# One transfer for the first tile's constants and filters, and a finer first operand, in a convolution and linear-layer kernel

## The reference, cut to what matters

```python
# layer 0: grouped 1-D convolution (4 groups, 9 taps) plus a context per channel, then a linear layer with low-rank experts
conv = conv1d(x, w[64, 16, 9], groups=4, pad=4) + (cond @ c_weight.T)[:, :, None] + fside[None, :, None]
x1   = x + conv @ W.T + b + best_expert(conv)         # W (1024, 1024); softmax gate over 4 ranks, top 1
# layer 1: per-sample mixture of 8 channel matrices, whose weights come from a small network on cond
att  = softmax(gelu(gelu(cond @ W0 + b0) @ W1 + b1) @ W2 + b2)
m    = einsum(att @ weight, x1) + att @ bias_k
out  = x1 + m @ W_base.T + b_base + sum_e sparsemax(router(m))_e * (m @ A_e) @ B_e
```

## Time and profile before

| | us |
|---|---|
| median of 3 runs | 518.55 |
| the runs | 518.16, 518.55, 519.62 |
| the profiled execution | 517.35 |
| its span, first to last instruction | 515.6 |
| PE busy in the span | 506.4 (98%) |
| DVE, ACT, POOL busy | 353.0, 131.4, 142.7 |

### The profile page before, as it was taken

The page is one execution under the profiler, slowest core; times in us unless marked ns, Lnnn a source line. Parts: engine busy times, 40 slices in busy tenths (PEclk is TensorE's granted clock), DMA queues, the critical chain, the costliest instruction groups (busy, mean ns, idle before and its releaser), DMA issues.

```text
span 515.6 us, 8706 instructions
## 1 busy us (share of the span) xinstructions
PE 506.4 (98%) x3227; PEld 478.1 (93%) x3227; DVE 353.0 (68%) x764; ACT 131.4 (25%) x271; POOL 142.7 (28%) x122
## 2 busy tenths in 40 slices
PE   7999999999999999999999899999999999999997
PEld 7999999999999999999999789999999999999986
DVE  2866988847676675766797586685748568584852
ACT  2741343312223122331352221111112111111200
POOL 1000010004443141433113372441606244060620
PEclk9999999999999999999999999999999999999999
DMA  7943404427377564647797952333415233430312
GB/s 273 349 133 125 134 1 135 160 90 239 131 249 229 203 234 158 211 151 258 257 421 268 402 181 85 121 105 127 140 60 165 82 120 106 132 136 18 104 43 81
DMA packets 41382, 85.32 MB, mean 165 GB/s; under 512 B 4059, under 2 KB 25051, under 8 KB 41340
## 3 DMA queue, kind: packets, MB, share of 16 engines
q1 hardware_dynamic: 31884, 61.38, 35.3%
q10 hardware_dynamic: 9456, 23.38, 12.2%
HBM read 59.30 MB, written 25.44 MB: 164 GB/s over the span
## 4 chain that ended last, share of the span: by engine, by line
PE 87%; DMA 7%; DVE 4%; issue 1%; SPq 1%; ACT 0%; POOL 0%; DVEq 0%; ACTq 0%
PE b_x L1178 6%; PE b_x L1180 6%; PE b_x L1181 6%; PE b_m L1129 5%; PE b_p L1162 4%; PE b_p L1164 4%; PE b_p L1163 4%; PE b_y L1178 4%; PE b_y L1181 4%; PE b_y L1180 4%; DMA x_scratch<-xs 4%; PE b_m L1139 2%; PE b_y L1129 2%; PE b_w L1180 2%; PE b_w L1178 2%; PE b_w L1181 2%
## 5 line engine op out<-in xcount | busy, mean ns | idle before, releaser
L530 ACT CAST a_hi<-mixed 128x512 fp32r<-128x512 f32 x64 | 38.7, 620 | 167.1 <-DVE mixed L812 91.8
L479 POOL TENSOR_TENSOR xs<-xs,mixw_sb 128x464 f32<-128x464 f32 (+1 forms) x32 | 45.1, 1419 | 123.7 <-DMA xs<-x_scratch 123.7
L824 DVE TENSOR_TENSOR s_lo<-mixed,s_hi 128x512 fp32r<-128x512 f32 x56 | 64.9, 1180 | 16.6 <-ACT s_hi L542 14.7
L1163 PE MATMUL b_p<-wp_lo,a_hi 128*128 128x232 f32 (+1 forms) x224 | 61.5, 275 | 0.0
L1162 PE MATMUL b_p<-wp_hi,a_hi 128*128 128x232 f32 (+1 forms) x224 | 61.4, 274 | 0.0
L1164 PE MATMUL b_p<-wp_hi,a_lo 128*128 128x232 f32 (+1 forms) x224 | 61.4, 274 | 0.0
L905 DVE TENSOR_TENSOR xs<-b_x,xs 128x464 f32<-128x464 f32 (+1 forms) x58 | 36.1, 622 | 31.1 <-PE b_x L1181 23.9
L542 ACT CAST s_hi<-mixed 128x512 fp32r<-128x512 f32 x56 | 34.8, 622 | 75.8 <-POOL mixed L452 36.2
L817 DVE TENSOR_TENSOR a_lo<-mixed,a_hi 128x512 fp32r<-128x512 f32 x64 | 48.0, 775 | 8.9 <-ACT a_hi L530 8.2
L452 POOL TENSOR_TENSOR mixed<-mixed 128x512 f32<-128x512 f32 x13 | 16.8, 1295 | 118.0 <-DVE a_lo L817 118.0
L1178 PE MATMUL b_x<-wb_hi,s_hi 128*128 128x464 f32 (+1 forms) x112 | 43.0, 384 | 1.7 <-DVE xs L905 1.7
(11 more groups left out here) (237 smaller groups left out, 1198.5 us busy)
## 6 DMA issues: line engine op xcount, KB each, us to landing
blk<-x_scratch SPq DMA_DIRECT2D x16, 512.0 KB, 3.5
blk<-in_xblk SPq DMA_DIRECT2D x15, 516.0 KB, 3.7
xs<-in_x SPq DMA_DIRECT2D x16, 296.0 KB, 4.3
x_scratch<-xs SPq DMA_DIRECT2D x16, 296.0 KB, 3.5
xs<-x_scratch SPq DMA_DIRECT2D x16, 280.0 KB, 3.3
out_dram<-xs SPq DMA_DIRECT2D x16, 280.0 KB, 2.4
w_raw<-in_wcat SPq DMA_DIRECT2D x8, 546.0 KB, 9.9
praw<-in_wcat ACTq DMA_DIRECT2D x8, 464.0 KB, 5.1
```

Of the source, the lines that this page charges most:

```text
L479: pool.tensor_tensor(xs[s][:, a:b], xs[s][:, a:b], bbase[:, a:b], ALU.add).then_inc(x_biased[q], 1)
L530: act.copy(a_hi[:, op, :, :], mixed[:, op, :, :]).then_inc(ahi_done[op], 1)
L824: dve.tensor_tensor(s_lo[:, i, :, :], mixed[:, S_AT[i], :, :], hi(s_hi[:, i, :, :]), ALU.subtract).then_inc(slo_done[i], 1)
L1163: pe.matmul(dst, x_hi, wp_lo[:, k, 0:PLAIN[l]], start=False, stop=False)
```

## The change

- The row constants (now replicated to 128 rows on the host), the contexts' inputs and all filters become one array `front`, 1204 float32 (4816 bytes) on each of 128 partitions, 616 thousand bytes. SP loads it in one transfer, its first. The loads at L318, L319, L321 and L620 go.
- `blk` of tile 0 is loaded whole (4128 bytes a partition) by ACT, as its first transfer; L320 and L322 go from SP's queue. SP's second transfer is now weight chunk 0.
- PE: `keep_warm(11)` in front instead of 7, none between the context product and the convolution, 2 instead of 3 ahead of the weights. The convolution of tile 0 waits for the whole front and the whole `blk`.
- DVE: the large lo part of weight chunk 0 is made ahead of the first context sum, the small one behind it. The second context sum of tile 0 is two operations of 256 elements, one for A11 and one for A12.
- ACT: weight chunks 0 and 1 are both cast ahead of A11. A11 is cast in two pieces, block 0 (128 elements) and blocks 1 to 3 (384 elements). `dense0(0, 0)` waits only for the first piece, `dense0(0, 1)` for both.

```diff
-WARM, WARM_CTX, WARM_WEIGHTS = 7, 1, 3
+WARM, WARM_WEIGHTS = 11, 2
...
+FR_C = ROW
+FR_CW = FR_C + NB
+FR_TAPS = FR_CW + CH
+FRONT = FR_TAPS + GROUPS * 2 * P
...
+        first_in = sb("first_in", [P, FRONT])
+        rw = first_in[:, 0:ROW]
+        filt = first_in[:, FR_TAPS:FRONT].rearrange("p (g c) -> p g c", g=GROUPS)
...
-            sp.dma_start(pk[:, 0:PK_W0], pack[:, 0:PK_W0]).then_inc(s_pk, 16)
-            sp.dma_start(filt[:, 0:half, :], taps[:, 0:half, :]).then_inc(s_filt[0], 16)
-            sp.dma_start(blk[0][:, 0:GROUPS * QX], xblk[0][:, 0:GROUPS * QX]).then_inc(blk_first, 16)
-            sp.dma_start(filt[:, half:, :], taps[:, half:, :]).then_inc(s_filt[1], 16)
-            sp.dma_start(blk[0][:, GROUPS * QX:], xblk[0][:, GROUPS * QX:]).then_inc(blk_loaded[0], 16)
+            sp.dma_start(first_in[:, :], front).then_inc(s_front, 16)
...
-            sp.dma_start(pk[:, PK_W0:], pack[:, PK_W0:]).then_inc(s_mlp, 16)
+            sp.dma_start(pk[:, :], pack).then_inc(s_mlp, 16)
...
-            act.dma_start(rw[:, :], rows.partition_broadcast(P)).then_inc(s_rw, 16)
+            act.dma_start(blk[0][:, :], xblk[0]).then_inc(blk_loaded[0], 16)
             act.dma_start(bk[:, :], bias_k).then_inc(s_bk, 16)
             split_w(0)
-            split_a(A11, 0)
             split_w(1)
+
+            act.wait_ge(sum_done, 1)
+            act.wait_ge(first_sum, 1)
+            act.copy(a_hi[:, A11, 0, :], mixed[:, A11, 0, :]).then_inc(first_hi, 1)
+            act.copy(a_hi[:, A11, 1:, :], mixed[:, A11, 1:, :]).then_inc(ahi_done[A11], 1)
             split_a(A12, 0)
...
-            dve.wait_ge(s_pk, 16)
+            dve.wait_ge(s_front, 16)
...
             dve.wait_ge(ctx_sum, 1)
+            split_w_main(0)
             sum_mix(0, 0)
-            sum_mix(0, 1)
-            split_w(0)
+            split_w_plain(0)
+
+            dve.wait_ge(mix_done, 2)
+            for q in (A11, A12):
+                dve.tensor_tensor(mixed[:, q, :, CH:P],
+                                  mix_bank(0, 1)[:, 4 * CH * q:4 * CH * (q + 1)].rearrange("p (a c) -> p a c", c=CH),
+                                  ctx_row[:, 0:1, CH:P].to_broadcast([P, HK, CH]),
+                                  ALU.add).then_inc((first_sum, sum_done)[q], 1)
             split_a(A11, 0)
             split_w(1)
             split_a(A12, 0)
...
-                if kc == 0:
+                if T == 0 and k == 0:
+                    pe.wait_ge(first_hi, 1)
+                elif kc == 0:
+                    pe.wait_ge(ahi_done[op], g + 1)
+                if T == 0 and k == 1:
                     pe.wait_ge(ahi_done[op], g + 1)
...
-            keep_warm(WARM_CTX)
+            pe.wait_ge(s_front, 16)
             conv_half(0, 0, b_m)
             conv_half(0, 1, b_w)
-            pe.wait_ge(s_pk, 16)
...
+    front = np.concatenate([np.tile(rows, (P, 1)), a["cond_128"].T, a["L0_cond_c_weight"].T,
+                            taps.reshape(P, GROUPS * 2 * P)], axis=1)
```

More of the change, by code:

```diff
@@ L61 @@
 EMB = 128
-WARM, WARM_CTX, WARM_WEIGHTS = 7, 1, 3
-PK_C = 0
-PK_CW = PK_C + NB
-PK_W0 = PK_CW + CH
+WARM, WARM_WEIGHTS = 11, 2
+PK_W0 = 0
 PK_W1 = PK_W0 + EMB
@@ L83, in layer, with build @@
     return g // PAIRS
-def build(nc, x, xblk, taps, wcat0, bcat0, bias0, wcat1, bcat1, b_base, pack, rows, mixw, bias_k, out):
+def build(nc, x, xblk, front, wcat0, bcat0, bias0, wcat1, bcat1, b_base, pack, mixw, bias_k, out):
     x_t = x.rearrange("(t n) c h -> t (n c) h", n=2)
@@ L172, in build @@
         b_m, b_u = bank("b_m"), bank("b_u")
-        s_pk, s_mlp, s_rw, s_bk, s_mixw = sem("s_pk"), sem("s_mlp"), sem("s_rw"), sem("s_bk"), sem("s_mixw")
-        s_filt = [sem("s_filt0"), sem("s_filt1")]
+        s_front, s_mlp, s_bk, s_mixw = sem("s_front"), sem("s_mlp"), sem("s_bk"), sem("s_mixw")
         s_lb, s_bias0, s_bbase = sem("s_lb"), sem("s_bias0"), sem("s_bbase")
@@ L218, in build @@
         consts = sem("consts")
+        first_sum, first_hi = sem("first_sum"), sem("first_hi")
         ctx_terms, ctx_mm, ctx_sum = sem("ctx_terms"), sem("ctx_mm"), sem("ctx_sum")
@@ L727, in _, with split_w_main @@
         def _(dve):
-            def split_w(k):
+            def split_w_main(k):
                 i = (B11, B21)[k // HK]
@@ L733, in split_w, with split_w_plain @@
                                   hi(wb_hi[:, i:i + 2, k % HK, 0:h]), ALU.subtract).then_inc(wlo_done, 1)
+            def split_w_plain(k):
                 dve.wait_ge(whi_done, 2 * k + 2)
-                dve.tensor_tensor(wp_lo[:, k, 0:PLAIN[0]], w_raw[:, k, 2 * h:],
+                dve.tensor_tensor(wp_lo[:, k, 0:PLAIN[0]], w_raw[:, k, 2 * HALF[0]:],
                                   hi(wp_hi[:, k, 0:PLAIN[0]]), ALU.subtract).then_inc(wlo_done, 1)
+            def split_w(k):
+                split_w_main(k)
+                split_w_plain(k)
             def split_t(i, kc):
@@ L916, in take_plain @@
                                   ALU.add).then_inc(finq[s], 1)
[L919 removed]
+            dve.wait_ge(s_front, 16)
             dve.tensor_tensor(u_sb[:, :, :].rearrange("p t (n c) -> p (t n) c", c=CH),
[L921 to L922 removed]
+                              first_in[:, FR_CW:FR_CW + CH].unsqueeze(1).to_broadcast([P, 4, CH]),
+                              first_in[:, FR_C:FR_C + 4].unsqueeze(2).to_broadcast([P, 4, CH]), ALU.mult).then_inc(ctx_terms, 1)
             dve.wait_ge(ctx_mm, 1)
[L924 removed]
             dve.tensor_tensor(ctx_row[:, :, :].rearrange("p t (n c) -> p (t n) c", c=CH),
@@ L1117, in conv_half @@
                 s = T % 2
[L1118 to L1121, removed]
+                pe.wait_ge(blk_loaded[s], 16 * (T // 2) + 16)
                 for g in range(GROUPS):
@@ L1124, in conv_half @@
                     dst = dst_bank[:, :].rearrange("p (a c) -> p a c", c=CH)[:, :, g * GC:(g + 1) * GC]
-                    if T == 0 and n == 0 and g % 2 == 0:
-                        pe.wait_ge(s_filt[g // 2], 16)
                     for side in range(2):
@@ L1270, in network @@
                     pe.wait_ge(s_mlp, 16)
-                    mlp(0, pk[:, PK_C:PK_C + NB])
+                    mlp(0, first_in[:, FR_C:FR_C + NB])
                 if step == 1:
@@ L1325, in _ @@
                       start=True, stop=True).then_inc(ctx_mm, 1)
-            keep_warm(WARM_CTX)
+            pe.wait_ge(s_front, 16)
             conv_half(0, 0, b_m)
             conv_half(0, 1, b_w)
-            pe.wait_ge(s_pk, 16)
             pe.wait_ge(ctx_sum, 1)
-            pe.matmul(b_z[0:NB, 0:CH], pk[:, PK_C:PK_C + NB], pk[:, PK_CW:PK_CW + CH],
+            pe.matmul(b_z[0:NB, 0:CH], first_in[:, FR_C:FR_C + NB], first_in[:, FR_CW:FR_CW + CH],
                       start=True, stop=True).then_inc(ctx_mm, 1)
@@ L1457, in _layout @@
     bias0[0] = bias0[-1] = a["L0_ffn_b"]
-    pack = np.concatenate([a["cond_128"].T, a["L0_cond_c_weight"].T, a["L1_cond_W0"], a["L1_cond_W1"],
-                           a["L1_cond_W2"], a["L1_cond_b0"][:, None], a["L1_cond_b1"][:, None]], axis=1)
+    pack = np.concatenate([a["L1_cond_W0"], a["L1_cond_W1"], a["L1_cond_W2"],
+                           a["L1_cond_b0"][:, None], a["L1_cond_b1"][:, None]], axis=1)
     rows = np.concatenate([a["fside_S_0"], a["L0_ffn_gate_b"], a["L1_cond_b2"], a["L1_ffn_b_router"]])
+    front = np.concatenate([np.tile(rows, (P, 1)), a["cond_128"].T, a["L0_cond_c_weight"].T,
+                            taps.reshape(P, GROUPS * 2 * P)], axis=1)
     mixw = np.zeros((2, OQ, KMIX, MIXES, 2, CH), np.float32)
@@ L1466, in _layout @@
     mixw = mixw.reshape(P, MIXES, 2 * CH)
-    return {"x": x, "xblk": xblk, "taps": taps, "wcat0": wcat0, "bcat0": bcat0, "bias0": bias0, "wcat1": wcat1,
-            "bcat1": a["L1_ffn_lora_B"].reshape(P, D), "b_base": a["L1_ffn_b_base"], "pack": pack, "rows": rows,
+    return {"x": x, "xblk": xblk, "front": front, "wcat0": wcat0, "bcat0": bcat0, "bias0": bias0, "wcat1": wcat1,
+            "bcat1": a["L1_ffn_lora_B"].reshape(P, D), "b_base": a["L1_ffn_b_base"], "pack": pack,
             "mixw": mixw, "bias_k": a["L1_cond_bias_k"]}
```

4 lines of the change are left out of this document (removed).

## The result

The changed kernel takes 515.99 us (median of 22 runs, 514.81 to 519.7) against 518.23 us (median of 22 runs of the kernel before on the same chips, 516.42 to 521.16). The ratio is 0.9961, interval 0.9946 to 0.9976: faster by 0.4%, 2.2 us, where 0.4 us was forecast; the time lies 0.6 us under the range. A second set of 12 runs of it gave 515.96 and 0.996 (0.9934 to 0.9986). The profiled executions differ by less, 515.9 (span 514.2) against 517.35 (span 515.6): 1.45 us.

The account below looks back on a forecast made before the run. PE was taken to bound the kernel, busy 506.4 of 515.6 us. F = 6.2 gave F − 6.63 = −0.4 us, so 517.35 − 0.4 = 516.95 profiled, plus 1.20 to the median: 518.15 us, range 516.6 to 520.0.

Parts of the forecast that it names:

- F: Landing of the front transfer, which everything stands behind: taken as 6.2 us; the time changes by F − 6.63 us.
- the moved split: DVE's large lo part of chunk 0 ahead of the first sum: free if the chunk lands by F + 1.75; expected F + 1.35.
- far end: Upper case for the front's landing: the slow DMA start of the kernel before repeats, giving F = 8.5.
- near end: Lower case for the front's landing: transfers of this shape on idle engines, F = 6.0 or 6.4.
- the way from the A11 sum to chunk 1's lo part: DVE and ACT from tile 0's A11 sum to chunk 1's lo part end: 3.45 us against 3.84, saving 0.4.
- whatever the end of chunk 1's lo part moves by, the end of the kernel moves by: From tile 1's convolution on PE does not stop, so the start's shift reaches the end whole, if later inputs are ready.
- The prediction's own sign: A span that moves by more than tile 1's convolution moves was to show the forecast wrong.
- the 1.20 us from the profiled execution to the median: Added to the profiled execution's forecast of 516.95 us to give the median of 518.15 us.
- something else moves: Rival: PE's waits behind 120 us shift, either way, by 2 us or so: 516.5 or 520.5 us; chance 0.13.
- The 4 added warm matmuls lie in time in which PE waits for F anyway: PE's start: the added warm matmuls cost nothing unless the front lands before 5.4 us.
- With both queues in use no slice passes 428 GB/s: Reading of the before trace: queues share the DMA engines, so `blk` on ACT's queue brings no extra bandwidth.
- the fit that the prediction took from the Trainium skill: First transfers: 2.0 us plus bytes over 436 GB/s, giving 4.6 us for the pair, F = 5.4, gain 1.2 us.

Follow-up runs that it names:

- order-only kernel: The kernel before with the changed kernel's DVE and ACT order and pieces, its own transfers and warm matmuls kept: 518.85 us, ratio 1.0017 (0.9999 to 1.0036).
- transfers-only: The changed kernel with its transfers and warm matmuls, but the DVE and ACT order, whole sum and whole cast of before: 516.74 us, ratio 0.9967.
- seven-warm: The changed kernel with 7 warm matmuls in front in place of 11: 517.8 us, ratio to before 0.9997 (0.9968 to 1.0026).
- plain-rows: The kernel before with the row constants stored as 128 rows in HBM instead of one row broadcast in the read: 517.22 us, ratio 0.998.
- broadcast-back: The changed kernel with the old broadcast read issued by ACT ahead of `blk`, into an unused tile: 523.49 us (6 runs), ratio to before 1.0103.
- before again: The kernel before, unedited, run again for a second profiled execution: 517.46 us.
- after again: The changed kernel, unedited, run again for a second profiled execution and more times: 515.96 us, ratio to before 0.996 (0.9934 to 0.9986).
- `blk` on SP: The changed kernel with tile 0's `blk` issued by SP right behind the front instead of by ACT: 516.21 us, ratio to before 0.9967 (0.9941 to 0.9992).
- Closing the gap of before: The kernel before with 4 warm matmuls between context product and convolution in place of 1: 517.34 against 519.23 us, ratio 0.9971 (0.9948 to 0.9995).
- the candidate: The changed kernel with `blk` on SP behind the front, first context sum ahead of chunk 0's split, small lo part behind the second sum: 515.37 us, ratio 0.9939.
- widened before: The kernel before without its one warm matmul between context product and convolution: 519.36 against 518.75 us, ratio 1.0007 (0.9984 to 1.0029).

## Why the prediction was wrong, step by step

**Right.** PE bounds the kernel, and tile 1's convolution follows the end of chunk 1's lo part: both moved by 1.13 us, and up to 132 us PE kept that shift whole (−1.15 to −1.18). The context product took 6.85 − 6.31 = 0.54 us (0.5 forecast), the convolution started at 6.85 = F + 1.04 (F + 1.03), and the moved split was free: DVE's first split started at 8.38 (limit 9.5), and DVE then waited only 0.27 us, for PE. That this holds only while the chunk comes early was right too, by the order-only kernel.

**Mis-sized: F.** 6.2 was forecast, 5.81 measured (5.79 again; 5.69 and 6.02 in the transfers-only and seven-warm kernels, whose first transfers are the same). The forecast stood between transfers on idle engines and the ramp of the kernel before, and no row said what made that ramp. The plain-rows and broadcast-back kernels say it: mainly the broadcast read, though with it F was 6.7 and not the 8.5 of the far end. Without it the near end holds (6.0) and a little more. Worth 0.4 us.

**Mis-sized: the way from the A11 sum to chunk 1's lo part.** 3.45 forecast, 3.23 measured. Up to the start of `a_lo` it was 1.26 us (10.62 to 11.88) for the 1.30 of the sum. The difference lies behind it: `a_lo` and chunk 1's lo parts took 1.97 us (11.88 to 13.85) where their durations sum to 2.13, because each operation's row starts before the row ahead of it has ended (`a_lo` from 11.88 for 0.69, chunk 1's large lo part at 12.49). The rows of before had the same overlap, 4.26 us of durations in 3.84 us, and the prediction called it small and left it out of the new sum. The A11 sum itself started at 10.62 instead of F + 4.90 = 10.71. Worth 0.3 us. Together: −0.4 − 0.4 − 0.3 = −1.1, which is the 1.13 us of the traces.

**Failed: "whatever the end of chunk 1's lo part moves by, the end of the kernel moves by".** The sum put everything behind the start at nothing. F and the way alone would have left it at 518.55 − 1.1 = 517.4, inside its range; it left the range by this step and by the next. The prediction's own sign says so: the span moved by more than tile 1's convolution, by 1.46 us (514.16 against 515.62) where the convolution moved by 1.13. The 6.3 us of idle time behind 120 us are not spread either: in before 2.7 us lie around the turn of the layers near 293 us, and 3.4 follow PE's last matmul. The turn moved. PE's windows around it, in before, before again, after, after again:

```profile
280.00:320.00 40.00, 37.33 (x221) 33.82 (x220) 28.37 (x50) 9.94 (x18) 17.45 (x12) 1.00 0.67 253
```
```profile
280.00:320.00 40.00, 37.30 (x219) 33.63 (x218) 28.11 (x49) 9.96 (x18) 17.47 (x12) 1.00 0.67 250
```
```profile
280.00:320.00 40.00, 38.03 (x224) 34.39 (x223) 25.98 (x49) 9.66 (x17) 16.91 (x12) 1.00 0.64 241
```
```profile
280.00:320.00 40.00, 37.95 (x223) 34.40 (x223) 26.00 (x48) 9.54 (x17) 16.83 (x12) 1.00 0.63 237
```
PE stands 2.7 us there in before, twice, and 2.0 in after, twice, and the shift goes from −0.73 to −1.35 and from −1.06 to −1.69 across it: 0.6 us that the sum lacked. Elsewhere after lost a little. In its first profile PE waits at 141 us for DVE, which it doesn't do in before, and the shift falls from −1.18 to −0.70; in the second it falls by 0.1:

```profile
141.22 1.86 PEld L1139 LDWEIGHTS b_z<-first_in,blk 128*128 128x128 f32 x16 [0.55 <-DVE xs L914]
```
What at the turn makes PE wait less in after isn't settled; the kernels with the new transfers stand 1.6 to 2.2 us there, the seven-warm one with its late start too (1.7), except broadcast-back (2.8) and `blk` on SP (3.8, with the clock fallen); those with the old transfers stand 2.5 to 2.7, and with the new order alone it is 3.2.

**Failed: the 1.20 us from the profiled execution to the median.** The forecast of 518.15 carried them over from 3 runs of before; in after the median is 0.09 us above the profiled execution. That is half of the miss of 2.16 us, and the profiled execution (516.95 forecast, 515.9 measured) the other half. With 22 runs the 1.20 is 0.88 in before, so one profile of each kernel shows 0.8 us less than the medians do. Fewer executions with a fallen clock in after are one reason, told next; the rest can be the choice of executions.

**Partly right: the rival "something else moves".** It was given 0.13 and had 2 us either way with nothing but the waits for it. It names the waits, not the clock, which has a part of its own: the mean granted clock that each run lists is below 0.9985 in 46 of the 104 runs of before that list one, which take 519.6 us on average against 517.9 for the others, and in 5 of 34 of after.

**Wrong, though not what the sum missed: "The 4 added warm matmuls lie in time in which PE waits for F anyway".** They do lie there, but what they prevent has a price. The sum counted on them for the context product's 0.5 us and gave the convolution its full pace, and both came true; it saw no cost beyond that without them. Taking four matmuls away from after costs 2.1 us at the start of the trace and 1.8 us of the median (516.0 to 517.8). Closing the gap of before brought about 0.3%, just clear of nothing. The Trainium skill, page TensorE: Matmul & The Clock Gate, section "HAM oscillation — how this bites in real kernels", tells of a wait for a DMA after which PE starts slow again. The trace agrees in the broadcast-back kernel, whose last warm loads took 0.11 us each and whose matmuls after the wait for `blk` took 3.75 us for 16 at a clock of 0.50. The seven-warm kernel is another case, since it was slow from its first load on. The same page of the Trainium skill says that a kernel shows a different number of slow first matmuls from one execution to the next. The warm loads agree, since the kernels give PE the same work up to there: the same 22 took 4.71 us in after (4.77 again), 4.35 in transfers only, 3.89 in the candidate.

**Two readings of the prediction that don't hold.** "With both queues in use no slice passes 428 GB/s" rests on a trace in which ACT's queue carried 44 KB, all but done when the rate was high. The trace of after does show it: with the front and `blk` in flight in two queues no slice up to their landings passes 403 GB/s. And the fit that the prediction took from the Trainium skill, page DMA: Bandwidth & Descriptors, stands there in the section "Anatomy of one DMA — SWDGE (gpsimd) path": it is for transfers on GpSimd's path, while this kernel's are issued by SP and ACT. The estimate by it was F = 5.4; measured was 5.81.

**Where the 2.2 us are.** The means of the runs that list a clock are 518.67 before (104) and 516.51 after (34). More runs of before with a fallen clock: the means of the runs above 0.9985 alone differ by 517.93 − 516.10 = 1.8, so about 0.3. That 1.8 is near what the profiled executions, whose clock at the turn had not fallen, show: their spans are 515.6 and 515.7 before, 514.2 and 513.8 after, 1.7 apart on average. Of it the start is 1.0 to 1.1 and the turn 0.6 to 0.7, less the 0.1 to 0.5 at 141 us. A start that is slow in some executions of before isn't needed for this account and isn't shown; 3 of the 29 runs of after with a full mean clock took 519.1 to 519.7 us too, and what slowed them has no records. The interval of the ratio is 0.8 us either way, so nothing finer can be read from the times.

## What to carry to other kernels

A wait of PE for its first inputs isn't free time: fill it with matmuls until the real ones start, and judge that by medians, because one profile can show the lucky execution. A change at the start can move a wait far behind it: compare the same instruction at several places of both traces, not at the start alone. Replicate small constants in HBM rather than broadcast them in the read, above all ahead of the first large loads. Here work moved ahead of a queue's urgent operation lost time without the transfer that brings its input early; time both, and each alone.

## What the runs showed of the hardware

- A read of one HBM row (336 bytes) into 128 partitions took 5.0 us in before and 6.1 in the broadcast-back kernel, 2.1 with 128 rows in HBM, and slowed the transfers of the other queue too: 48 to 92 GB/s instead of 184 to 324 between 2 and 4.5 us.
- The granted clock reads 1.00 from the first microsecond, while 128-wide loads take 0.22 us and later ones 0.12. It reads 1.00 from 7 to 11 us in the seven-warm kernel too, where 16 matmuls took 3.39 us. The end of the slow time, an estimate from the 22 warm loads at these two paces, was about 3.9 us in the candidate and 4.9 in transfers only; in after all 22 were slow, up to 5.8 us.
- In the broadcast-back kernel PE was fast from 4.2 us, waited 1.99 us and after a short product 1.78 us more, and then ran at a granted clock of 0.50. In the seven-warm kernel it was slow, waited 2.08 us and stayed slow until about 10.6 us. In the widened before it was slow, waited 1.52 us and was then fast, in its one profile.
- At the turn of the layers the clock fell in some executions of one kernel and not in others; it fell in the profiled ones of plain rows and of `blk` on SP (0.52), of the closed and the widened gap (0.53) and of broadcast-back (0.71), and not in the other nine. In plain rows and `blk` on SP the shift lost 1.2 and 3.4 us across the turn, the longer wait of PE in the latter included.
